# Folded attention inside a twelve-stage kernel: the order of TensorE's two projection operations, and ScalarE in place of VectorE for the normalisation

## What is computed

```
def _layernorm(x, axis=-1, eps=1e-05):
    m = jnp.mean(x, axis=axis, keepdims=True)
    v = jnp.var(x, axis=axis, keepdims=True)
    return (x - m) / jnp.sqrt(v + eps)

def _L2_attn_ref(x, Wq, bq, Wk, bk, Wv, bv, temperature):
    b, t, d = x.shape
    h = temperature.shape[0]
    dh = d // h
    q = (x @ Wq + bq).reshape(b, h, dh, t)
    k = (x @ Wk + bk).reshape(b, h, dh, t)
    v = (x @ Wv + bv).reshape(b, h, dh, t)
    attn = jnp.einsum('bhdt,bhds->bhts', k, v) * temperature
    attn = jax.nn.softmax(attn, axis=-1)
    out = jnp.einsum('bhdt,bhts->bhds', q, attn)
    return out.reshape(b, t, d)
```

## Time and profile before

| | us |
|---|---|
| median of three runs | 3638.08 |
| lowest and highest | 3636.49, 3638.13 |
| the profiled execution, its own time | 3631.84 |
| its span | 3629.9 |
| TensorE busy in the span | 3268.1 (90%) |
| VectorE busy | 2528.6 (70%) |
| ScalarE busy | 1815.8 (50%) |
| GpSimd busy | 1241.1 (34%) |

### The profile page before, as it was taken

One profiled execution on the slowest core, in us unless ns is written; L12 is line 12 of the kernel. 1 busy time (PEld: TensorE's weight loads), 2 busy tenths in 40 slices (PEclk: granted clock), 3 DMA queues, 4 the chain that ended last, 5 costly groups with the idle time before them and its releaser, 6 DMA issues. The chain is left out here.

```text
span 3629.9 us, 108450 instructions
## 1 busy us (share of the span) xinstructions
PE 3268.1 (90%) x40814; PEld 2730.2 (75%) x40816; DVE 2528.6 (70%) x7254; ACT 1815.8 (50%) x4530; POOL 1241.1 (34%) x1823
## 2 busy tenths in 40 slices
PE   5887899999989999897899999999999999774866
PEld 4776899999967777545788998898999898643345
DVE  6784899999968888657455655555655555478765
ACT  3331787877757777574433333333333333224463
POOL 4562888888833333303300000000000000155032
PEclk8996999999999999898799999999999999877677
DMA  4001000000022222200365554555555555264000
GB/s 122 1 0 38 1 0 0 0 0 0 1 64 79 78 78 79 57 1 7 87 129 132 132 130 122 139 128 133 131 131 123 138 127 133 67 113 71 0 3 26
DMA packets 375492, 254.10 MB, mean 70 GB/s; under 512 B 118676, under 2 KB 371560, under 8 KB 374536
## 3 DMA queue, kind: packets, MB, share of 16 engines
q1 hardware_dynamic: 370824, 245.44, 28.0%
q10 hardware_dynamic: 4352, 4.20, 0.5%
HBM read 233.53 MB, written 15.75 MB: 69 GB/s over the span
## 5 line engine op out<-in xcount | busy, mean ns | idle before, releaser
L2462 PE MATMUL psum<-L_xattn_ctxT,L_xattn_q_ctx 128*128 128x257 f32 x2048 | 511.2, 390 | 2.1 <-DMA L_xattn_ctx<-ctx_dram 2.1
L1061 PE MATMUL psum<-L_ffn_share,L_ffn_prob 128*128 128x128 f32 x4096 | 487.9, 278 | 23.2 <-DVE L_ffn_prob L994 15.2
L878 POOL TENSOR_TENSOR L_ffn_sums<-L_ffn_sims 128x1024 f32<-128x1024 f32 x256 | 485.0, 1911 | 61.4 <-DVE L_ffn_prob L994 61.4
L2493 PEld LDWEIGHTS psum<-L_xattn_probT,L_xattn_ctx 32*128 32x128 f32 x16384 | 468.9, 187 | 44.6 <-issue 42.0
L1061 PEld LDWEIGHTS psum<-L_ffn_share,L_ffn_prob 128*128 128x128 f32 x4096 | 471.3, 193 | 35.9 <-DVE L_ffn_prob L994 25.7
L2493 PE MATMUL psum<-L_xattn_probT,L_xattn_ctx 32*128 32x128 f32 x16384 | 493.2, 273 | 2.1 <-DVE L_xattn_probT L2376 2.1
L2314 ACT ACTIVATE L_xattn_prob<-psum,L_xattn_nmax 128x258 f32<-128x258 f32 x512 | 238.8, 471 | 478.7 <-DVE L_xattn_nmax L2362 462.0
L2285 POOL TENSOR_TENSOR L_xattn_z_var<-L_xattn_z_mv,L_xattn_z_eps 128x1 f32<-128x1 f32 x32 | 6.1, 190 | 1248.4 <-DVE L_xattn_z_mv L2388 1219.1
L2462 PEld LDWEIGHTS psum<-L_xattn_ctxT,L_xattn_q_ctx 128*128 128x128 f32 x2048 | 369.0, 191 | 64.3 <-issue 5.5
L920 ACT ACTIVATE psum<-L_ffn_sums,L_ffn_bias 128x512 f32<-128x512 f32 x512 | 339.1, 686 | 63.6 <-DVE L_ffn_prob L994 58.7
L994 DVE SCALAR_TENSOR_TENSOR L_ffn_prob<-L_ffn_sums,L_ffn_best,psum 128x512 f32<-128x512 f32 x512 | 358.4, 742 | 6.9 <-ACT psum L920 3.8
(11 more groups left out here) (459 smaller groups left out, 6567.2 us busy)
## 6 DMA issues: line engine op xcount, KB each, us to landing
L_xattn_ctx<-ctx_dram SPq DMA_DIRECT2D x512, 256.0 KB, 3.9
L_xattn_ctxT<-ctx_T_dram SPq DMA_DIRECT2D x128, 257.0 KB, 3.2
L_xattn_k_all<-ctx_T_dram SPq DMA_DIRECT2D x128, 128.5 KB, 2.1
L_xattn_v_all<-ctx_dram SPq DMA_DIRECT2D x128, 128.0 KB, 2.2
L_attn_qkv_scratch<-L_attn_qkv SPq DMA_DIRECT2D x24, 256.0 KB, 2.8
L_attn_rows<-L_attn_qkv_scratch SPq DMA_DIRECT2D x24, 256.0 KB, 5.3
start_raw<-ctx_dram ACTq DMA_DIRECT2D x16, 256.0 KB, 11.8
L_xattn_v_rows<-L_xattn_v SPq DMA_DIRECT2D x8, 256.0 KB, 2.3
```

Source lines behind the costliest of these rows:

```text
L878: nc.gpsimd.tensor_tensor(sums[:, h % RING, :, :], sx, sy, ALU.add).then_inc(summed, 1)
L1061: last = nc.tensor.matmul(pair(2 * s)[:, c * P:(c + 1) * P], prob[:, h % RING, c * P:(c + 1) * P], share[:, h % RING, :], start=(h == 0 an ...
L2462: last = nc.tensor.matmul(scores(s)[:, g, 0:CTX], q_ctx[:, p, c, b, h:h + 4, :].rearrange("p h n -> p (h n)"), ctxT[:, b, c, :], start=(c ...
L2493: last = nc.tensor.matmul(mix_bank(r)[:, c * P:(c + 1) * P], ctx[rows, b, k, c * P:(c + 1) * P], probT[rows, b % 2, k, :, :].rearrange("p ...
```

## The change

GpSimd makes a second factor for each tile, -mean x rstd (a drain and a `tensor_scalar` on one column). ScalarE normalises the tile as `Identity(rstd * x + shifted_mean)` into the same buffer `xn`, and in its program this stands behind the copy of the tile before. VectorE no longer normalises and no longer waits for GpSimd. TensorE's step has the transposition of tile t ahead of the projection of tile t-1.

```diff
+        shifted_mean = sb("shifted_mean", [P, W])
+        centred = core.sem(f"{name}_centred")
...
         @block.gpsimd
         def _(pool):
-            def rstd(t, j, live):
+            def normal_factors(t, j, live):
                 if live(-1):
-                    front.pool_rstd(pool, t + 1 - (j + 1) % W, only=(j + 1) % W)
+                    s = (j + 1) % W
+                    front.pool_rstd(pool, t + 1 - s, only=s)
+                    pool.drain()
+                    nc.gpsimd.tensor_scalar(shifted_mean[:, s:s + 1], front.mv[:, s, 0:1], front.rstd[:, s, :], -1.0, ALU.mult,
+                                            ALU.mult).then_inc(centred, 1)
...
-            pipelined(pool, W, -1, 0, rstd)
+            pipelined(pool, W, -1, 0, normal_factors)
...
         @block.scalar
         def _(act):
             def turn_copy(t, j, live):
-                front.act_copy(act, t - j, only=j)
+                if live(0):
+                    front.act_copy(act, t - j, only=j)
+                if live(-1):
+                    s = (j + 1) % W
+                    act.wait_ge(centred, t + 2)
+                    nc.scalar.activation(front.xn[:, s, :], core.x[:, ds(t + 1, 1), :].rearrange("p a d -> p (a d)"),
+                                         ACT.Identity, bias=shifted_mean[:, s:s + 1],
+                                         scale=front.rstd[:, s, :]).then_inc(front.normed, 1)
...
-            pipelined(act, W, 0, 0, turn_copy)
+            pipelined(act, W, -1, 0, turn_copy)
...
         @block.vector
         def _(dve):
             def project(t, j, live):
-                if live(-1):
-                    front.dve_normalise(dve, t + 1 - (j + 1) % W, only=(j + 1) % W)
                 if live(-2):
                     front.dve_moments(dve, t + 2 - (j + 2) % W, only=(j + 2) % W)
...
         @block.tensor
         def _(pe):
             def project(t, j, live):
+                if live(0):
+                    front.pe_transpose(pe, t - j, only=j)
                 if live(1):
...
                     nc.tensor.matmul(bank_b(s)[:, 0:3 * D], front.xnT[:, s, :], w[:, :], start=True,
                                      stop=True).then_inc(projected, 1)
-                if live(0):
-                    front.pe_transpose(pe, t - j, only=j)
```

## The result

The changed kernel took 3612.86 us, the median of four runs (3608.36 to 3616.82), against 3637.28 for the kernel before beside it: a ratio of 0.9931, with a 95% interval of 0.9916 to 0.9947. In a second comparison it took 3612.21 (five runs) against 3634.56, a ratio of 0.9937 (0.9923 to 0.9951). The two together are nine runs, 3608.36 to 3616.82, median 3612.2.

A forecast was written before the change was run, and what follows sets the result against it. Phase one was taken as bound by VectorE waiting for GpSimd (2.07 us) at full clock, TensorE's copy cycle (2.28) at half. Phase one's 19.8 us plus 1.0 in phase two, 20.8 off 3638.08, gave 3617.3 us, range 3612 to 3627.

The forecast's parts named there:

- start low, then full: TensorE's clock in phase one: half for four tiles or so, then lasting full clock; 3617 us, chance 0.52.
- The sum: Phase one: first bias at 6.45, 4 x 1.80 + 27 x 1.49, less 1.0: 52.9 us against 72.67.
- Phase two's start: First scores until VectorE's first reduction, 2.1 us at half clock, take about half at full clock: 1.0 us more gained.
- The cycle over four steps: Phase one, moments through factors, normalise, transposition, projection and bias: 4.48 + P = 4P, a step of 1.49 us at full clock.
- GpSimd's bound: GpSimd's two factors in phase one: at least 1.31 us a tile, the period taken from the third stage.
- ScalarE's tables: Rival in phase one: alternating Identity and Copy reload tables, 3.76 us a tile, 3686 us; 0.04 together with other such costs.
- The transfers: Rival: phase two waits for phase one's stores; at 107 GB/s 7.9 MB take 74 us, gain nil, 3638 us; chance 0.05.
- The half-clock step: TensorE's projection plus transposition a tile at half clock: 1.62 to 1.83 us, taken as 1.80.
- The standstill of the earlier trace is gone: TensorE in phase one: with the new order it projects during ScalarE's copy; the half-clock cycle of 2.28 us becomes 1.80.
- the busy share rises at either clock: Argument against a low or swinging clock in phase one: TensorE 81% busy at full clock, from 59% before.

The follow-up runs named there:

- one more addition: Changed kernel plus a one-column GpSimd addition a tile, into a tile nobody reads, between the two factors: 3617.28 us, one run.
- longer lead: Changed kernel with the moments three tiles ahead of the tile TensorE transposes, instead of two: 3608.32 us, then 3610.14 against the changed kernel's 3612.21.
- ScalarE alone: Changed kernel with TensorE's projection put back ahead of the transposition: ratio 0.9966 to the kernel before; five runs 3612.54 to 3615.57 us, five 3632.37 to 3640.32.
- spare matmuls: ScalarE alone plus five spare 128x384 TensorE matmuls before the phase's first transposition: 3615.38 us, then 3612.06; the same matmuls in the kernel before: 3636.84.
- the order alone: Kernel before with only the transposition moved ahead of the projection, VectorE still normalising: 3632.37 us against 3636.47, ratio 0.9988.

## Why the prediction was right

It said 3617 us, 3612 to 3627, and faster with 0.90. The time of 3612.9 lies at the low end of the range, and the likeliest case (start low, then full) is what the trace shows. The medians fell by 24.4 and 22.4 us in the two comparisons, where 20.8 were forecast; the stage accounts for 21.3 in the profiles, and the rest is no more than the spread of whole times (the kernel before took 3625 to 3645 us over all its runs).

*The sum.* 52.9 us were predicted for phase one, 52.5 and 52.3 measured, but errors in its terms cancelled, so that its closeness is in part luck. First bias: 6.45 predicted, 3170.47 - 3164.27 = 6.20 measured. First four steps: 7.2 predicted, 1.50 + 1.49 + 1.61 + 1.45 = 6.05 measured. The other 27, less the end: 39.2 predicted, 40.3 measured. Phase two's start: 1.0 predicted; up to the first reduction's start it took 3230.61 - 3228.45 = 2.16 us before and takes 3218.03 - 3216.78 = 1.25 now, 0.91 less, and phase two as a whole 1.17 less.

*The cycle over four steps* was right in its form; "4.48 + P, and it must be 4P" says 4.48 us for three steps. The round above is 4.62. Two terms were mis-sized: I gave each release 0.04 us, and ScalarE starts 0.12 behind the factors and the bias 0.15 behind the end of the projection's record, 0.19 more together; the projection follows 0.20 behind the transposition's start, not 0.25. The pattern of three unequal steps, the one more addition (once in three steps) and the longer lead each show that it is a cycle of waits over three steps.

*GpSimd's bound* of 1.31 was right as a bound (1.34 with the loop), and was not what bound. *ScalarE's tables*: L2690 ran 32 times at a mean of 493 ns with no table load beside it. *The transfers* moved 229 GB/s in 3188 to 3194 and held up nothing: in phase two the only one of the computing engines that waited for one was VectorE, before the last additions, 5.2 us where it was 5.3.

*The half-clock step* of 1.80 us was too long for the first tiles: it was "nearer the whole record", but records overlap. In the changed kernel's timeline:

```profile
3169.67 0.42 PE L166 MATMUL psum<-const,L_attn_front_xn_sb 128*128 128x128 f32 x1
...
3169.88 1.49 PE L2776 MATMUL psum<-L_attn_w,L_attn_front_xnT_sb 128*128 128x384 f32 x2
...
3171.16 0.42 PE L166 MATMUL psum<-const,L_attn_front_xn_sb 128*128 128x128 f32 x1
```

From start to start it is 0.21 + 1.28 = 1.49 us, and TensorE has no gap. Whether a long stretch at the half clock would have kept 1.5, or come to the 1.77 of my cycle, no run shows, since none of the changed kernel's profiles stayed there.

*The step that failed* is "The standstill of the earlier trace rows is gone", as a gain. I worked out the old order's cycle at the half clock alone (2.28) and never at the full clock with ScalarE normalising. There it is 1.44, under the 1.54 of the new cycle, and the reversal, which makes each projection wait for one more tile, gains nothing. The 20 us need VectorE's normalisation gone and the full clock. The order's part is to make the clock come, which I had not counted on. My argument for the clock, "the busy share rises at either clock", is not enough either. At the full clock it rose to 70% (4.19 of 6 us), not to the 81% of my sum, which added up records that overlap. And the long execution of ScalarE alone stood at 81% and stayed low, the short one went to 69% and stayed high. The Trainium skill, "TensorE: Matmul & The Clock Gate", Part 1, which I had cited for the release, also says that the moment of the release varies between runs of one kernel. These runs go further: with the old order it varied whether the release came in the phase at all (six of eleven).

What stays open: what told the two groups apart. Nothing in this stage's records did for the first 6.2 us, and before them TensorE had stood idle for 11.52 us in the long execution and 11.71 in the short one. That gapless work at the start brings the full clock is shown by counts (nine runs of the changed kernel, ten with spare matmuls, against six of eleven), not by a mechanism. The other runs with ScalarE normalising add to the counts: ten with the new order and the longer lead (3604.75 to 3614.05 us), one with the addition, and four with the old order, spare matmuls and the longer lead (3610.48 to 3615.86), all short. All five long runs came from one chip. On that chip five of the ten with the longer lead and the one with the addition ran too, and none of the six was long; the spare matmuls ran only on two others, where ScalarE alone ran once, so for them a difference between chips is not ruled out.

## What to carry to other kernels

Before crediting a reordering, work out the cycle that it breaks for the kernel as it will be, at each clock it may run at: here another edit had already brought the broken cycle below the one that took its place. A step longer than any engine's own work is a cycle of waits; follow it once round in the timeline, divide by the steps that it spans, and lengthen its lead by one tile. Make a stage that starts after a pause give TensorE work without gaps, and measure more than one run: one profile of ScalarE alone would have shown either no gain or all of it.

## What the hardware showed that I had not expected

With one program, TensorE's clock took two courses from starts that look the same: 0.50 for 60 us at 81% busy in one execution, 1.00 at 69% busy in another; the means of the two groups, 3614.3 and 3637.7 us, are 23 us apart. In the kernel before with spare matmuls the full clock came and went again within the phase, after 15.5 us at 62% busy; without them it did so too, at 1.00 in 3182 to 3192 and 0.50 behind it. And in the kernel with the order alone, steps of 2.07 us took the same time at either clock, so a low clock there cost nothing.
